# A strided write moves from ScalarE's side of a buffer to VectorE's: key squares and key sum in a quaternion memory kernel

## The chip, the cores and the metric

The kernel runs on one core of a Trainium2 chip. The metric is the device time of one launch, in microseconds. Three runs of the kernel before gave 640.27 us (median; 639.76 to 642.27).

## The reference

Two batches of 4096 tokens with 256 channels pass through three blocks, each adding to the residual: half a feed-forward block, a memory block, and half a feed-forward block again. Of the memory block, cut to what matters here:

```python
keys = (x @ Wk.T + bk).reshape(B, L, 64, 4)              # 64 quaternions of 4 components
knorm = jnp.linalg.norm(keys, axis=-1, keepdims=True)    # root of the sum of the 4 squares
keys = keys / jnp.maximum(knorm, 1e-12)
values = (x @ Wv.T + bv).reshape(B, L, 64, 4)
memory = jnp.cumsum(quat_mul(values, keys), axis=1)      # prefix sum over the tokens
retrieved = quat_mul(memory, quat_conj(keys)).reshape(B, L, D)
retrieved = retrieved / jnp.sqrt(positions)
normed = (retrieved - mean) / jnp.sqrt(var + 1e-5) * ln_g + ln_b   # over the 256 channels
return x + (normed @ Wo.T + bo)
```

## The kernel before

The residual stays in the on-chip memory `res` for the whole run. A feed-forward stage over blocks of 512 tokens comes first, then the memory stage, then a second feed-forward stage. The change is in the memory stage.

The memory stage works in **steps** of 256 tokens (two tiles of 128 tokens, `i` = 0 and 1), alternating between the batches `b` = 0 and 1. Step s = 2j + b; there are 32 of them, s = 0 to 31. `rounds` writes the first four and the last four out and runs the 24 between, s = 4 to 27, in a hardware loop of two steps an iteration. Weights are laid out by component on the host, so the 256 channels of a key stand as four runs of 64: all first components, then all second ones, and so on.

Each engine runs its own list of instructions in order, with semaphores between them. The lists are written out by hand in `body` of each engine; nothing reorders them. In one step, with the line of each:

- TensorE makes the keys and values (L1369) of the step after, the prefix sums of this step (L1398, L1405), and transposes and the output product of the step before (L1414, L1425).
- ScalarE, in `body` under `mem`: copies the key bias (L919), the transposed input (L908), `normedT` (L954) and the value bias (L924), adds the normalized input (L900), squares the keys (`key_square`, L930, `ksq`), takes the layer norm's standard deviation (`std`, L882, `n_std`), takes the norm of the keys (`key_norm`, L937 and L940), and normalizes (L891, L947).
- VectorE, in `body` under `mem`: unit keys (`key_unit`, L616, `khat`), products of tile 0 (`bind`, L622, written to `xn`), retrieval products of tile 0 (`retrieve`, L622, written to `gating_buffers`), statistics of the step before (`ln_stats`, L582), `bind` of tile 1, `own_stats` (L595, L596: a wait for its own statistics, carried by a write of one column that nobody reads), `ln_moments` (L587, two aggregations into `n_mv`), `key_sum` (L603, `ksum`), `store_x` (L659), `ln_inverse` (L592, `n_rstd`), `retrieve` of tile 1, `key_inverse` (L609, `kinv`).
- GpSimd adds the products up, twelve additions a step (L267 to L294).

`ksq` is laid out with the four components of a quaternion beside each other. ScalarE reads the keys component by component and so writes every fourth word of `ksq`, 16 bytes apart; `key_sum` reads it straight through, four words to a sum.

The links that matter: `key_sum` waits for `ksq_done` from ScalarE; `std` on ScalarE waits for `mv_done` from `ln_moments`; `ln_inverse` on VectorE waits for `std_done`, and `retrieve` of tile 1 stands behind it. ScalarE runs `key_square`, `std`, `key_norm` in that order. Steps 1 and 2 have no `store_x`.

Of the kernel before, what the change touches and what calls it, by code (L numbers as in the profile page):

```python
# [21 lines left out]
ALU = mybir.AluOpType  # L22
ACT = mybir.ActivationFunctionType

P = 128
# [5 lines left out]
def need(engine, semaphore, count):  # L31

    if isinstance(count, int) and count <= 0:
        return
    engine.wait_ge(semaphore, count)
# [34 lines left out]
def at(j, b, d):  # L70

    return j + (b + d) // 2, (b + d) % 2


def macaron(nc, x, w_kv, w_o, w_r, w_k, w_v, columns, out):
# [3 lines left out]
    Q = D // 4  # L79
# [8 lines left out]
    with ExitStack() as ctx:  # L88
        def sb(name, shape, dt=F32):
            return ctx.enter_context(nc.sbuf_tensor(name, shape, dt))  # L90

        def sem(name):
            return ctx.enter_context(nc.semaphore(name))
# [70 lines left out]
        n_rstd = sb("n_rstd", [P, 2, 2])  # L164
        m_xn = sb("m_xn", [P, 2, D])
        m_xnT = sb("m_xnT", [P, FC, 2 * P])
        ksq = sb("ksq", [P, 2, Q, 4])
        ksum = sb("ksum", [P, 2, Q])
        above = sb("above", [P, 2, Q])
        knorm = sb("knorm", [P, 2, Q])  # L170
# [21 lines left out]
        keys = bank[0][:, 1, :].rearrange("p (t n) -> p t n", t=2)  # L192
# [45 lines left out]
        m = {n: sem(f"m_{n}") for n in MEM_SEMS}  # L238
# [110 lines left out]
        def _(dve):  # L349
# [208 lines left out]
            def mem():  # L558

                def x_variance(n, first, end):  # L560
                    dve.wait_ge(m["x_moments_done"], 2 * (end // CT))
                    nc.vector.tensor_scalar(x_var[:, :, first:end], x_moments[:, :, first:end, 1], LN_EPS, None,
                                            ALU.add).then_inc(m["x_var_done"], 1)

                def x_scales(n, first, end):
                    if n == 0:
                        dve.wait_ge(m["x_power_done"], 1)
                    else:
                        dve.wait_ge(m["x_std_done"], n)
                        nc.vector.reciprocal(x_rstd[:, :, first:end], x_std[:, :, first:end]).then_inc(m["x_rstd_done"], 1)  # L570
                        dve.wait_ge(m["x_rstd_done"], n)
                    nc.vector.tensor_scalar(x_gain[:, :, first:end], x_rstd[:, :, first:end], 1.0, None, ALU.add)
                    nc.vector.scalar_tensor_tensor(x_shift[:, :, first:end], x_moments[:, :, first:end, 0], -1.0,
                                                   x_rstd[:, :, first:end], ALU.mult, ALU.mult).then_inc(m["x_scales_done"], 1)


                def ln_stats(j, b):
                    s = 2 * j + b
                    need(dve, m["normed_done"], s - 1)
                    for i in range(2):  # L580
                        dve.wait_ge(ret_done[i], s + 1)
                        nc.vector.bn_stats(n_st[:, b, i, :], ret[:, b, i, :]).then_inc(m["st_done"], 1)  # L582

                def ln_moments(j, b):
                    s = 2 * j + b
                    for i in range(2):
                        last = nc.vector.bn_aggr(n_mv[:, b, i, :], n_st[:, b, i, :])  # L587
                    last.then_inc(m["mv_done"], 1)

                def ln_inverse(j, b):  # L590
                    dve.wait_ge(m["std_done"], 2 * j + b + 1)
                    nc.vector.reciprocal(n_rstd[:, b, :], n_std[:, b, :]).then_inc(m["rstd_done"], 1)  # L592

                def own_stats(j, b):
                    dve.wait_ge(m["st_done"], 2 * (2 * j + b) + 2)  # L595
                    nc.vector.memset(spare[:, :], 0.0)  # L596

                def key_sum(j, b):

                    s = 2 * j + b  # L600
                    dve.wait_ge(m["ksq_done"], s + 1)
                    need(dve, m["above_done"], s)
                    nc.vector.tensor_reduce(ksum[:, :, :], ksq[:, :, :, :], mybir.AxisListType.X, ALU.add).then_inc(m["ksum_done"], 1)  # L603

                def key_inverse(j, b):
                    s = 2 * j + b
# [13 lines left out]
                def all_products(dst, b, i, of, done):  # L620

                    nc.vector.tensor_tensor(  # L622
                        dst[:, i, :, :].rearrange("p (a b) n -> p a b n", a=4),
                        of.rearrange("p (a n) -> p a n", n=Q).unsqueeze(2).to_broadcast([P, 4, 4, Q]),
                        khat[:, b, i, :].rearrange("p (b n) -> p b n", n=Q).unsqueeze(1).to_broadcast([P, 4, 4, Q]),
                        ALU.mult).then_inc(done, 1)

                def bind(j, b, i):
                    s = 2 * j + b
                    dve.wait_ge(m["khat_done"], s + 1)  # L630
                    dve.wait_ge(m["V_done"], s + 1)
                    need(dve, bound_done[i], s)
                    all_products(bprod, b, i, values[b][:, i, :], bprod_done[i])

                def retrieve(j, b, i):
                    s = 2 * j + b
                    need(dve, ret_done[i], s)
                    dve.wait_ge(upto_done[i], s + 1)
                    all_products(rprod, b, i, memory[b], rprod_done[i])

                def first_inverse():
                    key_sum(0, 0)
                    key_inverse(0, 0)
# [10 lines left out]
                def store_x(j, b):  # L654
                    s = 2 * j + b
                    dve.wait_ge(m["O_done"], s + 1)
                    dve.wait_ge(m["res_done"], s + 1)
                    t = tiles(b * NT + j * 2, 2)
                    nc.vector.tensor_tensor(t, o_bank, t, ALU.add).then_inc(m["x_done"], 1)  # L659

                def body(j, has, next_stats, next_scales, next_difference):
                    for b in range(2):
                        behind = has(b, -1)
                        if not has(b, 1):

                            retrieve(j, b, 0)
                            store_x(*at(j, b, -3))
                            next_stats(1)
                            retrieve(j, b, 1)
                            ln_stats(*at(j, b, -1))  # L670
                            own_stats(*at(j, b, -1))
                            ln_moments(*at(j, b, -1))
                            store_x(*at(j, b, -2))
                            ln_inverse(*at(j, b, -1))
                            next_difference()
                            continue
                        last_but_one = has(b, 1) and not has(b, 2)
                        if has(b, -1) and not has(b, -2):
                            x_variance(2, NT - CT, NT)
                        if has(b, -2) and not has(b, -3):  # L680
                            x_scales(2, NT - CT, NT)
                        if has(b, 1):
                            key_unit(*at(j, b, 1))
                            bind(*at(j, b, 1), 0)
                        retrieve(j, b, 0)
                        if last_but_one:
                            next_scales(0)
                        if behind:
                            ln_stats(*at(j, b, -1))
                        if has(b, 1):  # L690
                            bind(*at(j, b, 1), 1)
                        if behind:
                            own_stats(*at(j, b, -1))
                            ln_moments(*at(j, b, -1))
                        if has(b, 3) and not has(b, 4):
                            next_stats(0)
                        if has(b, 2):
                            key_sum(j + 1, b)
                        if has(b, -3):
                            store_x(*at(j, b, -3))  # L700
                        if behind:
                            ln_inverse(*at(j, b, -1))
                        retrieve(j, b, 1)
                        if has(b, 2):
                            key_inverse(j + 1, b)
# [58 lines left out]
        def _(act):  # L764
# [109 lines left out]
            def mem():  # L874
# [51 lines left out]
                def key_square(j, b):  # L926
                    s = 2 * j + b
                    act.wait_ge(m["K_done"], s + 1)
                    need(act, m["ksum_done"], s)
                    nc.scalar.activation(ksq[:, :, :, :].rearrange("p t n c -> p t c n"), keys.rearrange("p t (c n) -> p t c n", n=Q),  # L930
                                         ACT.Square).then_inc(m["ksq_done"], 1)

                def key_norm(j, b):
# [633 lines left out]
```

## Time and profile before

| | value |
|---|---|
| Median of three runs | 640.27 us |
| Profiled execution: its own time | 642.52 us |
| Profiled execution: span | 640.8 us |
| Mean granted TensorE clock, share of full speed | 0.991 |
| TensorE busy, share of span | 612.2 us, 96% |
| VectorE busy | 561.6 us, 88% |
| GpSimd busy | 530.6 us, 83% |
| ScalarE busy | 467.8 us, 73% |

The shares are means over three different stages; a stage has to be read by itself. The memory stage lies between about 180 and 470 us of the span, its hardware loop between about 232 and 432 us. Records overlap a little: an instruction's record may start some 0.07 us before the one ahead of it ends, so what an instruction costs its engine is the distance between two starts, not its duration. The span is counted inside the device time, which is 1.7 us longer.

### The profile page before, as it was taken

The numbers are of one execution on the slowest core, as the hardware profiler recorded it, in microseconds if no ns is written. First come the engines' busy times: TensorE is split into PE (matmuls) and PEld (weight loads), VectorE is DVE, ScalarE is ACT, GpSimd is POOL, SyncE is SP. The second block draws the span as 40 slices with busy tenths as digits, with TensorE's granted clock in tenths as the row PEclk, the third lists the DMA queues.
The fourth block names the chain that finished last, engine by engine and source line by source line (L and its number), as shares of the span: only waits on it lengthen the run. The fifth ranks groups of instructions, "written<-read, shape, count | busy, mean of one in ns | idle before, by whom it ended". The sixth has DMA issues, their size and how long they took to land.

```text
span 640.8 us, 12174 instructions
## 1 busy us (share of the span) xinstructions
PE 612.2 (96%) x3294; PEld 517.5 (81%) x3295; DVE 561.6 (88%) x1170; ACT 467.8 (73%) x858; POOL 530.6 (83%) x616
## 2 busy tenths in 40 slices
PE   6899999999997899999999999998899999999997
PEld 4688989989875777877877778777678898898996
DVE  6699999998868999999999999999988788787773
ACT  5576777767656888888888888887476767777662
POOL 1589888887846999999999999998937988889863
PEclk8999999999998999999999999999899999999999
DMA  7840000000000000000000000000000111110221
GB/s 233 256 136 2 0 0 0 0 0 1 1 1 1 0 3 0 0 0 0 0 0 0 0 0 0 0 0 1 1 1 33 35 65 49 50 65 33 66 66 65
DMA packets 19273, 18.65 MB, mean 29 GB/s; under 512 B 1329, under 2 KB 19249, under 8 KB 19249
## 3 DMA queue, kind: packets, MB, share of 16 engines
q1 hardware_dynamic: 19248, 18.36, 8.8%
q8 instruction: 11, 0.18, 0.1%
q14 instruction: 14, 0.11, 0.1%
HBM read 9.97 MB, written 8.39 MB: 29 GB/s over the span
## 4 chain that ended last, share of the span: by engine, by line
PE 49%; POOL 25%; issue 18%; DVE 2%; ACT 2%; DMA 1%; POOLq 1%; SPq 0%; ACTq 0%; DVEq 0%
PE bank L1251 24%; PE bank L1292 17%; POOL rhalf L287 7%; POOL ret L294 6%; POOL kact L276 5%; POOL bhalf L269 4%; PE bank L1265 4%; PE bank L1425 1%; POOL bhalf L267 1%; PE bank L1311 1%; DMA wo<-w_o 1%; POOL rhalf L285 1%; ACT xn L794 1%; PE bank L1242 1%; POOL xr_lo L1108 1%
## 5 line engine op out<-in xcount | busy, mean ns | idle before, releaser
L1292 PE MATMUL bank<-wffn,kact 128*128 128x256 f32 x512 | 117.4, 382 | 4.8 <-DVE kact L425 2.8
L1369 PE MATMUL bank<-wkv,m_xnT 128*128 128x256 f32 x480 | 117.9, 389 | 2.1 <-ACT m_xnT L908 2.1
L301 POOL TENSOR_TENSOR xk_lo<-xk,xk_hi 128x1024 fp32r<-128x1024 f32 x30 | 71.1, 2370 | 47.7 <-ACT xk_hi L810 47.6
L1369 PEld LDWEIGHTS bank<-wkv,m_xnT 128*128 128x128 f32 x480 | 89.9, 192 | 24.3 <-ACT m_xnT L908 8.5
L1292 PEld LDWEIGHTS bank<-wffn,kact 128*128 128x128 f32 x512 | 94.8, 190 | 18.1 <-DVE kact L425 3.2
L1115 POOL TENSOR_TENSOR res<-res,gating_buffers 128x1024 f32 (+1 forms) x31 | 74.6, 2408 | 12.9 <-DVE gating_buffers L432 12.5
L622 DVE TENSOR_TENSOR xn<-bank,khat 128x1024 f32<-128x1024 f32 x64 | 77.7, 1216 | 2.2
L622 DVE TENSOR_TENSOR gating_buffers<-bank,khat 128x1024 f32<-128x1024 f32 x64 | 77.5, 1210 | 0.3 <-POOL ret L294 0.3
L1108 POOL TENSOR_TENSOR xr_lo<-xr,xr_hi 128x1024 fp32r<-128x1024 f32 x30 | 71.1, 2369 | 1.5
L1425 PE MATMUL bank<-wo_centred,normedT 128*128 128x256 f32 x256 | 67.7, 394 | 4.1 <-DVE res L659 2.1
L794 ACT ACTIVATE xn<-res,shift,rstd 128x256 f32 (+1 forms) x124 | 64.4, 594 | 4.6 <-POOL shift L1103 3.6
L1251 PE MATMUL bank<-wffn_hi,xr_hi 128*128 128x256 f32 x240 | 67.4, 281 | 0.0
L1251 PE MATMUL bank<-wffn_hi,xr_lo 128*128 128x256 f32 x240 | 67.4, 281 | 0.0
L1251 PE MATMUL bank<-wffn_lo,xr_hi 128*128 128x256 f32 x240 | 67.3, 280 | 0.0
L1425 PEld LDWEIGHTS bank<-wo_centred,normedT 128*128 128x128 f32 x256 | 44.6, 194 | 22.3 <-issue 14.0
L816 ACT CAST xr_hi<-xr 128x1024 fp32r<-128x1024 f32 x30 | 31.4, 1046 | 38.4 <-DVE xr L417 38.4
L267 POOL TENSOR_TENSOR bhalf<-xn 128x256 f32<-128x256 f32 x64 | 46.8, 731 | 11.2 <-DVE xn L622 11.1
L432 DVE TENSOR_TENSOR gating_buffers<-bank,gating_buffers 128x1024 f32<-128x1024 f32 x31 | 37.7, 1217 | 20.8 <-ACT gating_buffers L833 15.2
L407 DVE TENSOR_TENSOR diff<-bank,xnT 128x1024 f32<-128x1024 f32 x32 | 39.1, 1222 | 15.6 <-ACT xnT L785 15.4
L1251 PE MATMUL bank<-xk_hi,wffn_hi 128*128 128x512 f32 x120 | 50.1, 418 | 0.0
L285 POOL TENSOR_TENSOR rhalf<-gating_buffers 128x256 f32<-128x256 f32 x64 | 47.0, 734 | 2.2 <-DVE gating_buffers L622 2.1
L276 POOL TENSOR_TENSOR kact<-bhalf 128x256 f32<-128x256 f32 x64 | 47.5, 743 | 0.2
(140 smaller groups left out, 1602.0 us busy)
## 6 DMA issues: line engine op xcount, KB each, us to landing
res<-x SPq DMA_DIRECT2D x15, 512.0 KB, 4.2
out<-res SPq DMA_DIRECT2D x15, 512.0 KB, 2.9
res<-x SPq DMA_DIRECT2D x2, 256.0 KB, 2.9
out<-res SPq DMA_DIRECT2D x2, 256.0 KB, 2.1
wffn<-w_k SPq DMA_DIRECT2D x1, 256.0 KB, 5.3
wffn<-w_r SPq DMA_DIRECT2D x1, 256.0 KB, 6.0
wo<-w_o SPq DMA_DIRECT2D x1, 256.0 KB, 6.3
wffn<-w_v SPq DMA_DIRECT2D x1, 256.0 KB, 6.6
```

The lines of the kernel that those rows point to most:

```text
L267: engine.tensor_tensor(quarters(bhalf[:, i, 0, :]), picked(p, BIND_PLUS), picked(p, BIND_MINUS), ALU.subtract)
L276: engine.tensor_tensor(bound[:, b, i, :], bhalf[:, i, 0, :], bhalf[:, i, 1, :], ALU.add).then_inc(bound_done[i], 1)
L285: engine.tensor_tensor(quarters(rhalf[:, i, 0, :]), picked(p, RET_PLUS), picked(p, RET_MINUS), ALU.subtract)
L301: ops.tensor_tensor(xk_lo[:, :, :], xk[:, :, :], xk_hi[:, :, :].bitcast(F32), ALU.subtract).then_inc(e["xklo_done"], 1)
L622: nc.vector.tensor_tensor(dst[:, i, :, :].rearrange("p (a b) n -> p a b n", a=4), of.rearrange("p (a n) -> p a n", n=Q).unsqueeze(2).to_br ...
L794: last = nc.scalar.activation(xn[:, b, i, :], t[:, i, :], ACT.Identity, bias=shift[:, b, i:i + 1], scale=rstd[:, b, i:i + 1])
L1108: nc.gpsimd.tensor_tensor(xr_lo[:, :, :], xr[:, :, :], xr_hi[:, :, :].bitcast(F32), ALU.subtract).then_inc(e["xrlo_done"], 1)
L1115: nc.gpsimd.tensor_tensor(t, t, gated, ALU.add).then_inc(e["res_done"], 1)
L1251: last = nc.tensor.matmul(out_ap, w(f), v(f), start=k == 0, stop=k == n - 1)
L1292: last = nc.tensor.matmul(dst[:, i, :], x[:, f, i * P:(i + 1) * P], wffn[:, w, f, :], start=f == 0, stop=f == FC - 1)
L1369: last = nc.tensor.matmul(dst[:, i, :], m_xnT[:, f, i * P:(i + 1) * P], wkv[:, f, col:col + D], start=False, stop=f == FC - 1, skip_group_ ...
L1425: nc.tensor.matmul(o_bank[:, i, :], normedT[:, f, i * P:(i + 1) * P], wo_centred[:, f, :], start=f == 0, stop=False)
```

## The change

Three things change. `ksq` is laid out component by component: ScalarE now writes four runs of 64 words, and VectorE's reduction reads the four terms of a sum 64 words (256 bytes) apart. In the steps that have a `key_sum` (s = 0 to 29), VectorE runs it ahead of the two aggregations instead of behind them, and the wait for its own statistics stands in front of the sum. In these steps the write of one column (`own_stats`) is gone; steps 30 and 31 keep it.

```diff
--- before.py
+++ after.py
@@ -164,7 +164,7 @@
         n_rstd = sb("n_rstd", [P, 2, 2])
         m_xn = sb("m_xn", [P, 2, D])
         m_xnT = sb("m_xnT", [P, FC, 2 * P])
-        ksq = sb("ksq", [P, 2, Q, 4])
+        ksq = sb("ksq", [P, 2, 4, Q])
         ksum = sb("ksum", [P, 2, Q])
         above = sb("above", [P, 2, Q])
         knorm = sb("knorm", [P, 2, Q])
@@ -600,7 +600,7 @@
                     s = 2 * j + b
                     dve.wait_ge(m["ksq_done"], s + 1)
                     need(dve, m["above_done"], s)
-                    nc.vector.tensor_reduce(ksum[:, :, :], ksq[:, :, :, :], mybir.AxisListType.X, ALU.add).then_inc(m["ksum_done"], 1)
+                    nc.vector.tensor_reduce(ksum[:, :, :], ksq[:, :, :, :].rearrange("p t c n -> p t n c"), mybir.AxisListType.X, ALU.add).then_inc(m["ksum_done"], 1)
 
                 def key_inverse(j, b):
                     s = 2 * j + b
@@ -689,13 +689,17 @@
                             ln_stats(*at(j, b, -1))
                         if has(b, 1):
                             bind(*at(j, b, 1), 1)
+                        if has(b, 2):
+
+                            if behind:
+                                dve.wait_ge(m["st_done"], 2 * (2 * j + b - 1) + 2)
+                            key_sum(j + 1, b)
+                        elif behind:
+                            own_stats(*at(j, b, -1))
                         if behind:
-                            own_stats(*at(j, b, -1))
                             ln_moments(*at(j, b, -1))
                         if has(b, 3) and not has(b, 4):
                             next_stats(0)
-                        if has(b, 2):
-                            key_sum(j + 1, b)
                         if has(b, -3):
                             store_x(*at(j, b, -3))
                         if behind:
@@ -927,7 +931,7 @@
                     s = 2 * j + b
                     act.wait_ge(m["K_done"], s + 1)
                     need(act, m["ksum_done"], s)
-                    nc.scalar.activation(ksq[:, :, :, :].rearrange("p t n c -> p t c n"), keys.rearrange("p t (c n) -> p t c n", n=Q),
+                    nc.scalar.activation(ksq[:, :, :, :], keys.rearrange("p t (c n) -> p t c n", n=Q),
                                          ACT.Square).then_inc(m["ksq_done"], 1)
 
                 def key_norm(j, b):
```

On VectorE, from `bind` of tile 1 to `key_inverse` in the first step of the hardware loop, before (`xn` is what `bind` writes, `gating_buffers` what `retrieve` writes; ISA rows work out semaphore targets and addresses):

```order
L622 TENSOR_TENSOR xn<-bank,khat 128x1024 [waits m_bound1_done,m_V_done,m_khat_done]
L595 ISA
L596 MEMSET spare 128x1 [waits m_st_done]
L587 BN_AGGR n_mv<-n_st 128x2 x2
L601 ISA
L603 TENSOR_REDUCE ksum<-ksq 128x128 [waits m_above_done,m_ksq_done]
L656 ISA
L659 ISA [waits m_res_done,m_O_done]
L659 TENSOR_TENSOR res<-bank,res 128x512
L592 RECIPROCAL n_rstd<-n_std 128x2 [waits m_std_done]
```

And the same place now:

```order
L622 TENSOR_TENSOR xn<-bank,khat 128x1024 [waits m_bound1_done,m_V_done,m_khat_done]
L695 ISA
L601 ISA [waits m_st_done]
L603 TENSOR_REDUCE ksum<-ksq 128x128 [waits m_above_done,m_ksq_done]
L587 BN_AGGR n_mv<-n_st 128x2 x2
L656 ISA
L659 ISA [waits m_res_done,m_O_done]
L659 TENSOR_TENSOR res<-bank,res 128x512
L592 RECIPROCAL n_rstd<-n_std 128x2 [waits m_std_done]
```

The reduction has moved up past the two aggregations and directly behind the products, the column write has gone, and its wait (`m_st_done`) stands at an ISA row ahead of the reduction. Behind the aggregations only `store_x` (L659) is now left ahead of the reciprocal that waits for `m_std_done`. In the changed kernel lines behind the edit have numbers larger by 4.

## Rows read from the trace of the kernel before

**Rows 1.** Hardware loop: stretch, length, busy PE, PEld, DVE, ACT, POOL; clock, DMA share, GB/s.

```profile
232.00:432.00 200.00, 198.64 (x983) 159.78 (x982) 194.84 (x332) 170.66 (x353) 194.80 (x282) 1.00 0.00 0
```

**Rows 2.** Timeline of VectorE, one step: start us, duration us, instruction.

```profile
310.64 0.18 DVE L587 BATCH_NORM_AGGREGATE n_mv<-n_st 128x2 f32<-128x6 f32 x1
310.66 0.06 DVE L596 MEMSET spare<- 128x1 f32 x1
310.74 0.15 DVE L587 BATCH_NORM_AGGREGATE n_mv<-n_st 128x2 f32<-128x6 f32 x1
310.80 0.65 DVE L603 TENSOR_REDUCE ksum<-ksq 128x128 f32<-128x512 f32 x1
311.37 0.68 DVE L659 TENSOR_TENSOR res<-bank,res 128x512 f32 x1
311.97 0.15 DVE L592 RECIPROCAL n_rstd<-n_std 128x2 f32<-128x2 f32 x1
312.04 1.20 DVE L622 TENSOR_TENSOR gating_buffers<-bank,khat 128x1024 f32<-128x1024 f32 x1
313.16 0.94 DVE L609 RECIPROCAL kinv<-knorm 128x128 f32<-128x128 f32 x1
314.14 0.69 DVE L616 TENSOR_TENSOR khat<-bank,kinv 128x512 f32<-128x512 f32 x1
314.95 1.23 DVE L622 TENSOR_TENSOR xn<-bank,khat 128x1024 f32<-128x1024 f32 x1
316.09 1.22 DVE L622 TENSOR_TENSOR gating_buffers<-bank,khat 128x1024 f32<-128x1024 f32 x1
317.22 0.91 DVE L582 BATCH_NORM_STATS2 n_st<-ret 128x6 f32<-128x256 f32 x2
318.05 1.21 DVE L622 TENSOR_TENSOR xn<-bank,khat 128x1024 f32<-128x1024 f32 x1
319.18 0.18 DVE L587 BATCH_NORM_AGGREGATE n_mv<-n_st 128x2 f32<-128x6 f32 x1
```

**Rows 3.** Waits, 240 to 420 us: total us, times, longest us.

```profile
ACT bank L919 <- DVE khat L616: 16.8, 21, 0.8
...
POOL bhalf L267 <- DVE xn L622: 5.0, 22, 0.2
...
PEld bank L1369 <- ACT m_xnT L908: 3.9, 10, 0.4
```

**Rows 4.** Timeline of ScalarE in the same step; idle time before it in brackets.

```profile
309.60 1.13 ACT L930 ACTIVATE ksq<-bank 128x512 f32<-128x512 f32 x1
311.02 0.48 ACT L882 ACTIVATE n_std<-n_mv,eps_pos 128x1 f32<-128x1 f32 x2 [0.28 <-DVE n_mv L587]
311.49 0.40 ACT L937 ACTIVATE above<-ksum,minus_least 128x128 f32<-128x128 f32 x1
...
314.86 0.59 ACT L919 COPY bank<-kv_bias 128x512 f32<-128x512 f32 x1 [0.76 <-DVE khat L616]
```

**Rows 5.** Timeline of VectorE in step 1, which stores no block.

```profile
208.04 0.18 DVE L587 BATCH_NORM_AGGREGATE n_mv<-n_st 128x2 f32<-128x6 f32 x1
...
208.84 0.17 DVE L592 RECIPROCAL n_rstd<-n_std 128x2 f32<-128x2 f32 x1
```

**Rows 6.** ScalarE by line, whole run: busy us, mean ns of one; idle before.

```profile
L930 ACT ACTIVATE ksq<-bank 128x512 f32<-128x512 f32 x32 | 36.2, 1131 | 7.5 <-PE bank L1369 4.8 <-PE bank L1379 1.3
...
L785 ACT COPY xnT<-bank 128x1024 f32<-128x1024 f32 x32 | 32.5, 1016 | 1.7 <-PE bank L1275 0.5 <-PE bank L1265 0.3
...
L908 ACT COPY m_xnT<-bank 128x512 f32<-128x512 f32 x32 | 18.5, 580 | 1.4 <-PE bank L1362 1.4
```

**Rows 7.** VectorE by line, whole run.

```profile
L622 DVE TENSOR_TENSOR gating_buffers<-bank,khat 128x1024 f32<-128x1024 f32 x64 | 77.5, 1210 | 0.3 <-POOL ret L294 0.3
...
L603 DVE TENSOR_REDUCE ksum<-ksq 128x128 f32<-128x512 f32 x32 | 21.0, 656 | 5.6 <-ACT ksq L930 5.6
```

**Rows 8.** Waits of VectorE, whole run: total us, times, longest us.

```profile
DVE ksum L603 <- ACT ksq L930: 5.6, 2, 3.2
```

## Prediction

> **What bounds the kernel now.** I read the split by stretches first, since the change touches only the memory stage. In the 200 us of its hardware loop four engines look full [rows 1]: TensorE 198.64 us, GpSimd 194.80, VectorE 194.84; ScalarE, with 170.66, is the only one with room. Busy shares don't tell which of them paces, so next come the waits. Over 21 steps GpSimd waits for VectorE's products 22 times, 5.0 us in all, 0.23 us a step; ScalarE waits for the unit keys 21 times, 16.8 us, 0.8 us a step; TensorE's weight loads wait for ScalarE's copy, 3.9 us in all [rows 3]. No wait of VectorE is long enough to be listed. The timeline confirms it: from 310.64 to 319.18 VectorE starts one instruction after another, each at most 0.13 us after the end of the one ahead and most of them a little before it [rows 2]. So a step is 8.54 us long because VectorE's list is that long, and the loop has 24 steps. What lengthens VectorE's list by d costs 24 d there; what shortens ScalarE's buys nothing while it still waits 0.8 us a step. GpSimd follows closely: if VectorE were quicker, at most 0.23 us a step could be had before GpSimd paces.
>
> **The squares on ScalarE.** Writing every fourth word, the square of 128x512 takes 1131 ns; a copy of the same size out of PSUM that writes straight takes 580 ns [rows 6]. The new write is straight, so I expect about 590 ns, 0.55 us less on each of 32. In the loop this buys nothing: ScalarE's next instruction, the standard deviation, waits for VectorE's aggregations anyway (idle 0.28 us even now, [rows 4]). Where VectorE waits for the squares it is a gain: that happens twice, outside the loop [rows 8], so -1.1 us.
>
> **The sum on VectorE.** It now reads words 256 bytes apart. No row shows VectorE doing that, so its cost is bounded. Lower end: nothing, 656 ns as now [rows 7], if VectorE is held only by its count of elements; a gain is excluded, since count, output and engine are the same. Upper end: all that the same 512 elements cost ScalarE extra when they were 16 bytes apart, 1131 - 580 = 0.55 us [rows 6]. Between them stands a limit per access: ScalarE's straight word costs (1016 - 580) / 512 = 0.85 ns, its spaced word 0.85 + 551 / 512 = 1.93 ns [rows 6]. VectorE's straight word costs (1210 - 690) / 512 = 1.02 ns [rows 2, 7]. Were each spaced word to cost 1.93 ns here too, the sum would grow by 512 x 0.91 ns = 0.47 us. The nearest row is the spaced write, the only spaced access in the trace; I take 0.40 us, a little under, since VectorE reads four words for each that it writes while ScalarE wrote every one. Times 32 sums: +12.8 us. VectorE paces the 24 steps of the loop; in the eight sums outside it the sum stands on the path too, ahead of the key norm at the start and in a full list of VectorE elsewhere.
>
> The Trainium skill (Vector Engine (DVE) Microarchitecture Reference, Measured stream behaviour on trn2) speaks against this edit: a port streams at full rate only in runs of two adjacent words, and one source that hops at every element took 1.73 ns a column where contiguous ones took 1.054. An estimate by that is 512 x 0.68 ns = 0.35 us a sum, and the whole would come to 654.4 us instead of my 656. The same section has a one-source operation that alternates between two regions and still reads at full rate; by that one the sum would cost nothing. Neither was measured on a reduction, and no row here decides between them.
>
> **The order on VectorE, and the new wait.** Let R be the start of the sum. It takes the place of the first aggregation, 1.13 us behind the start of the second product (318.05 to 319.18, [rows 2]). It holds VectorE 0.57 us (310.80 to 311.37), each aggregation about 0.08, so `store_x` starts at R + 0.73 and the reciprocal `n_rstd` could start 0.60 later, at R + 1.33. That is what the list gives now as well: first aggregation to reciprocal 311.97 - 310.64 = 1.33. But the reciprocal waits for ScalarE's standard deviation, which waits for the second aggregation. Now the sum lies beside that round trip and hides it: from first aggregation to the end of the deviations 311.50 - 310.64 = 0.86 us [rows 2, 4]. After the change the first aggregation starts at R + 0.57; with 0.02 less for the column write and 0.04 for the release (314.10 to 314.14, `kinv` to `khat`) the reciprocal can't start before R + 0.57 + 0.86 - 0.02 + 0.04 = R + 1.45. So VectorE has a new wait of 0.12 us a step, and behind it stands `retrieve` of tile 1, then the reciprocal of the norms, `khat` and all of the next step: 24 x 0.12 = +2.9 us. A slower sum doesn't change this term, since it moves both sides.
>
> Steps 1 and 2 have no `store_x`. There first aggregation to reciprocal is 208.84 - 208.04 = 0.80 us [rows 5], already the round trip; with the sum ahead it becomes 0.57 + 0.80, so +0.57 us each, +1.1 us. In step 28 the statistics of the next stage stand between, and nothing is added. Steps 3 and 29 I put at nothing.
>
> **The column write.** Its record is 0.06 us, but the aggregations around it start at 310.64 and 310.74 [rows 2], so it holds VectorE 0.02 at most. In the loop that is already in the chain above, whose end decides. I cost it at nothing otherwise. Its wait for the statistics costs nothing either: these end before the second product starts, 1.13 us earlier.
>
> **What moves on the other engines.** The key norm gets its sum 0.16 us earlier but stands behind the deviations on ScalarE, which end later: 0.56 us later against the start of the product in the free case, and 0.96 with the slower sum, while `khat` itself moves by 0.12 or 0.52. ScalarE's 0.76 us of idle time ahead of the bias copy [rows 4] falls to about 0.3 in either case, so nothing behind it is late. The edit of the order pays back nothing there.
>
> **The sum.** 12.8 + 2.9 + 1.1 - 1.1 = +15.7 us. The profiled execution took 642.52 us itself (span 640.8 and 1.7 around it), so its like would take 658.2. It lies 2.25 us above the median of the three runs, 640.27; taken off, the forecast is 656.0 us, 2.5% slower.
>
> **The rivals.**
> 1. The spaced read is free. For it: an engine that takes one word a cycle may fetch far enough ahead; the spaced access that was slow was a write. Against it: the write was slowed to about twice. Left are 2.9 + 1.1 - 1.1 = +2.9 us, 643.2 us, +0.45%. That is so near the 0.5% (3.2 us) a measurement of this kernel can tell from no change that I split it two to one between same and slower.
> 2. The loop is paced by a ring and not by VectorE's list: unit keys, bias copy, transposed copy, key product, squares, key sum. For it: the squares end at 310.73, only 0.07 us ahead of the sum at 310.80 [rows 2, 4]. If that edge is the true limit, 0.55 us off the squares frees the step until GpSimd paces, which has 0.23 us to give [rows 3]: 24 x 0.23 = 5.5 us, and 634.8 us. It decides wherever VectorE idles ahead of the sum and the read is free. Against it: VectorE doesn't idle there, the aggregation ahead runs right up to the sum.
> 3. The spaced read costs far more than the spaced write did, 0.8 us a sum: 32 x 0.8 + 2.9 = +28.5, 668.8 us. Against it: no row has a word of 2.6 ns.
> 4. The order does not matter because ScalarE answers faster (its two deviations start at once): rival 1 or the forecast less 2.9 us, within their ranges.
>
> **Chances and range.** Forecast 0.57, rival 1 0.31, rival 2 0.05, rival 3 0.07. The likeliest case alone, with 0.25 to 0.55 us a sum, spans 8.0 to 17.6 us and the 2.9: 651 to 661 us. The range has to take in the free read and the upper bound: 641 to 662. From the cases: faster by over 0.5% 0.06, within 0.5% 0.22, slower 0.72.
>
> **What would show it.** In the changed profile: the squares at about 590 ns; the mean of the key sum, 656 ns if rival 1 holds, 1.0 to 1.1 us if I am right; idle time of VectorE ahead of `n_rstd` put down to ScalarE's deviations, about 0.1 us in each of 24 steps; step length 8.54 + 0.12 + 0.40 = 9.06 us in the loop (8.66 with a free read). GpSimd's wait for products should grow by the same amount a step. I am wrong if the key sum keeps its time, if no wait appears ahead of `n_rstd`, or if the step gets shorter than 8.54 us.

## The result, and the profile after

The changed kernel took 658.78 us (median of six; 656.92 to 661.98) against 640.43 us for six runs of the kernel before. The medians are 18.4 us apart, where 15.7 had been forecast. The ratio of the runs is 1.027, 95% interval 1.025 to 1.029, which is 17.2 us (15.8 to 18.6); 18.4 lies inside, and a remainder of a microsecond or two is not resolved by it. The profiled execution took 661.98 us itself, span 660.3, and is the slowest of the six; its mean granted clock was 0.982 where the other five had 0.988 or 0.989. That matters below.

The memory stage holds nearly all of it. From the start of the first `khat` to the start of the last it took 452.34 - 185.38 = 266.96 us before, and 470.54 - 184.53 = 286.01 us now. The hardware loop's 24 steps grew from 8.54 to 9.08 us each.

The loop's stretch in the changed profile, columns as in [rows 1]; it is now 219 us long:

```profile
232.00:451.00 219.00, 206.60 (x1019) 164.62 (x1018) 211.90 (x314) 160.31 (x362) 200.98 (x290) 1.00 0.00 0
```

ScalarE is down to 160.31 us in a longer stretch, GpSimd has 200.98 of 219; VectorE, with 211.90, is the fullest. One step of VectorE, which answers to [rows 2]:

```profile
318.67 1.04 DVE L603 TENSOR_REDUCE ksum<-ksq 128x128 f32<-128x512 f32 x1
319.64 0.23 DVE L587 BATCH_NORM_AGGREGATE n_mv<-n_st 128x2 f32<-128x6 f32 x2
319.80 0.65 DVE L659 TENSOR_TENSOR res<-bank,res 128x512 f32 x1
320.51 0.17 DVE L592 RECIPROCAL n_rstd<-n_std 128x2 f32<-128x2 f32 x1
320.60 1.22 DVE L622 TENSOR_TENSOR gating_buffers<-bank,khat 128x1024 f32<-128x1024 f32 x1
321.73 0.94 DVE L609 RECIPROCAL kinv<-knorm 128x128 f32<-128x128 f32 x1
322.71 0.69 DVE L616 TENSOR_TENSOR khat<-bank,kinv 128x512 f32<-128x512 f32 x1
323.52 1.23 DVE L622 TENSOR_TENSOR xn<-bank,khat 128x1024 f32<-128x1024 f32 x1
324.67 1.22 DVE L622 TENSOR_TENSOR gating_buffers<-bank,khat 128x1024 f32<-128x1024 f32 x1
325.80 0.91 DVE L582 BATCH_NORM_STATS2 n_st<-ret 128x6 f32<-128x256 f32 x2
326.62 1.21 DVE L622 TENSOR_TENSOR xn<-bank,khat 128x1024 f32<-128x1024 f32 x1
327.75 1.04 DVE L603 TENSOR_REDUCE ksum<-ksq 128x128 f32<-128x512 f32 x1
```

From sum to sum it is 327.75 - 318.67 = 9.08 us. The sum holds VectorE 0.97 us (318.67 to 319.64) instead of 0.57, and `store_x` to `n_rstd` is 0.71 us (319.80 to 320.51) instead of 0.60: the reciprocal waits. ScalarE in the same step, which answers to [rows 4]:

```profile
317.63 0.60 ACT L934 ACTIVATE ksq<-bank 128x512 f32<-128x512 f32 x1
320.00 0.48 ACT L886 ACTIVATE n_std<-n_mv,eps_pos 128x1 f32<-128x1 f32 x2 [1.76 <-DVE n_mv L587]
320.39 0.39 ACT L941 ACTIVATE above<-ksum,minus_least 128x128 f32<-128x128 f32 x1
...
323.44 0.59 ACT L923 COPY bank<-kv_bias 128x512 f32<-128x512 f32 x1 [0.44 <-DVE khat L616]
```

The squares are quick and buy nothing: they are followed by 1.76 us of waiting for the aggregations. The deviations end at 320.48, and `n_rstd` starts 0.03 us later. The idle time ahead of the bias copy fell from 0.76 us to 0.44, where the prediction had about 0.3. By line, the two operations whose access was exchanged, squares first ([rows 6, 7] before):

```profile
L934 ACT ACTIVATE ksq<-bank 128x512 f32<-128x512 f32 x32 | 19.2, 599 | 9.6 <-PE bank L1373 7.1 <-PE bank L1383 1.3
```

```profile
L603 DVE TENSOR_REDUCE ksum<-ksq 128x128 f32<-128x512 f32 x32 | 33.4, 1044 | 5.9 <-ACT ksq L934 4.6 <-issue 1.4
```

ScalarE gave back 1131 - 599 = 532 ns a step, VectorE's record grew by 1044 - 656 = 388 ns. Not all of the 388 is the read: the experiments show that some 20 ns come with the sum's new place. The waits, 240 to 430 us, against [rows 3]:

```profile
ACT n_std L886 <- DVE n_mv L587: 37.3, 21, 1.8
...
POOL bhalf L267 <- DVE xn L622: 15.8, 21, 0.8
...
PE bank L1429 <- DVE res L659: 8.7, 21, 0.4
```

GpSimd's wait for VectorE's products is up from 0.23 to 0.75 us a step, the 0.5 us by which the list of VectorE grew. TensorE now waits for `store_x` (L1429, 0.4 us a step), which it did not before; it costs nothing by itself, as the experiments leave no third term in the loop. VectorE's new wait ahead of `n_rstd` is too short for this view: outside steps 1 and 2 it shows only in the distances between starts, 0.71 against 0.60 us.

### The profile page after: what moved, and what is told of

It reads as the page before. It is cut to its first block, busy times and chain, and to the rows that moved or that the text cites. A ratio compares the mean times of both kernels' runs of the same rounds, so it can differ in the third digit from the quotient of the medians.

```text
span 660.3 us, 12145 instructions
## 1 busy us (share of the span) xinstructions
PE 620.1 (94%) x3294; PEld 521.2 (79%) x3295; DVE 576.6 (87%) x1141; ACT 447.7 (68%) x858; POOL 530.9 (80%) x616
## 4 chain that ended last, share of the span: by engine, by line
PE 47%; POOL 26%; issue 18%; DVE 4%; ACT 2%; DMA 1%; POOLq 1%; SPq 0%; DVEq 0%; ACTq 0%
PE bank L1255 23%; PE bank L1296 16%; POOL rhalf L287 6%; POOL bhalf L269 6%; POOL ret L294 6%; POOL kact L276 5%; PE bank L1269 4%; PE bank L1429 1%; POOL bhalf L267 1%; PE bank L1315 1%; POOL rhalf L285 1%; DMA wo<-w_o 1%; PE bank L1246 1%; DVE diff L407 1%; ACT xn L798 0%
## 5 line engine op out<-in xcount | busy, mean ns | idle before, releaser
L1373 PE MATMUL bank<-wkv,m_xnT 128*128 128x256 f32 x480 | 119.5, 393 | 4.6 <-ACT m_xnT L912 2.1
L1296 PE MATMUL bank<-wffn,kact 128*128 128x256 f32 x512 | 119.2, 387 | 4.8 <-DVE kact L425 2.8
L1429 PE MATMUL bank<-wo_centred,normedT 128*128 128x256 f32 x256 | 69.7, 403 | 13.2 <-DVE res L659 12.6
L1429 PEld LDWEIGHTS bank<-wo_centred,normedT 128*128 128x128 f32 x256 | 45.8, 199 | 31.7 <-issue 23.2
L407 DVE TENSOR_TENSOR diff<-bank,xnT 128x1024 f32<-128x1024 f32 x32 | 39.1, 1222 | 16.0 <-ACT xnT L789 15.8
L886 ACT ACTIVATE n_std<-n_mv,eps_pos 128x1 f32<-128x1 f32 x64 | 15.4, 287 | 55.4 <-DVE n_mv L587 55.3
```

The source lines that it names most:

```text
L407: nc.vector.tensor_tensor(diff[:, :, :], xT_ps, xnT[:, b, :, 0:CW], ALU.subtract).then_inc(e["diff_done"], 1)
L1296: last = nc.tensor.matmul(dst[:, i, :], x[:, f, i * P:(i + 1) * P], wffn[:, w, f, :], start=f == 0, stop=f == FC - 1)
L1373: last = nc.tensor.matmul(dst[:, i, :], m_xnT[:, f, i * P:(i + 1) * P], wkv[:, f, col:col + D], start=False, stop=f == FC - 1, skip_group_ ...
L1429: nc.tensor.matmul(o_bank[:, i, :], normedT[:, f, i * P:(i + 1) * P], wo_centred[:, f, :], start=f == 0, stop=False)
```

## Experiments

The theory after the result: the spaced read costs 0.39 us a sum and the new wait some 0.12 us a step, and the two add up. The rivals: the read alone does it; the order does most of it; an engine behind them paces. Loop steps below are the mean distance of the starts of `khat` over the 24 steps. Edits are shown shortened. The kernel before was run again beside each group of experiments: its median was 642.05 us (17 runs) beside the first four (layout, order, late reciprocal, pairs) and 641.00 us (23 runs) beside the others, against the 640.4 that the first expectations start from. The ratios are to these runs.

**The layout alone.**

```diff
-        ksq = sb("ksq", [P, 2, Q, 4])
+        ksq = sb("ksq", [P, 2, 4, Q])
-  tensor_reduce(ksum[:, :, :], ksq[:, :, :, :], X, ADD)
+  tensor_reduce(ksum[:, :, :], ksq[:, :, :, :].rearrange("p t c n -> p t n c"), X, ADD)
-  activation(ksq[:, :, :, :].rearrange("p t n c -> p t c n"), keys..., Square)
+  activation(ksq[:, :, :, :], keys..., Square)
```

> Only the layout of ksq is changed; order and column write as before. Theory (the spaced read costs 0.39 us a sum, the order a further 0.12 us a step): 640.4 + 32 x 0.39 - 1.1 for the faster squares = 651.8 us, key sum 1.04 us, no idle time ahead of n_rstd, loop step 8.54 + 0.39 = 8.93 us. Rival A (the spaced read alone makes all of the loss): 658.8 us. Rival B (the order makes most of it): under 648 us.

Measured: 652.77 us, ratio 1.015 (1.012 to 1.019); step 8.91 us, 0.37 above the kernel before. VectorE's timeline:

```profile
315.77 1.02 DVE L603 TENSOR_REDUCE ksum<-ksq 128x128 f32<-128x512 f32 x1
316.70 0.68 DVE L659 TENSOR_TENSOR res<-bank,res 128x512 f32 x1
317.30 0.16 DVE L592 RECIPROCAL n_rstd<-n_std 128x2 f32<-128x2 f32 x1
```

The sum is slow, and the reciprocal follows `store_x` after 0.60 us as before: no wait. The sum holds VectorE 0.93 us (315.77 to 316.70) in the place where it held it 0.57. Both rivals fall: the step carries 0.37 of the 0.54 us, neither all nor the smaller part, and 652.8 is neither 658.8 nor under 648.

**The order alone.**

```diff
-  own_stats; ln_moments; key_sum
+  wait st_done; key_sum; ln_moments          # in steps 0 to 29; layout of ksq as before
```

> Only the order on VectorE is changed and the column write left out; ksq laid out as before, squares 1.13 us, key sum 0.66 us. Theory: n_rstd waits for ScalarE's deviations, and the sum, now earlier, waits a little for the slow squares as well (they end 0.07 us ahead of its old place): loop step about 8.70 us, 24 x 0.16 + 1.1 for steps 1 and 2 = +5, 645.4 us. Rival A (the spaced read is all of the loss): 640.4 us or a little under, from the write that is gone.

Measured: 651.94 us, ratio 1.015 (1.012 to 1.019). The expectation was 6.5 us too low, 1.6 of which is the kernel before, which took 642.05 in this round and not 640.4. The step is 8.84 us, 0.30 more than before, and the place where it comes from is in VectorE's timeline:

```profile
322.73 1.21 DVE L622 TENSOR_TENSOR xn<-bank,khat 128x1024 f32<-128x1024 f32 x1
323.96 0.69 DVE L603 TENSOR_REDUCE ksum<-ksq 128x128 f32<-128x512 f32 x1
324.56 0.24 DVE L587 BATCH_NORM_AGGREGATE n_mv<-n_st 128x2 f32<-128x6 f32 x2
324.72 0.66 DVE L659 TENSOR_TENSOR res<-bank,res 128x512 f32 x1
325.45 0.17 DVE L592 RECIPROCAL n_rstd<-n_std 128x2 f32<-128x2 f32 x1
325.53 1.22 DVE L622 TENSOR_TENSOR gating_buffers<-bank,khat 128x1024 f32<-128x1024 f32 x1
```

Product to sum is 1.23 us (1.13 before): the sum waits for the slow squares. Sum to reciprocal is 1.49 us, 0.16 above the 1.33 of before. So the order costs more with the old layout than with the new, and the two costs do not simply add: 0.37 and 0.30 alone make 0.54 together, because the layout takes the wait for the squares away. The estimate of 0.16 a step was to hold both waits, which measure 0.10 and 0.16; the last 0.04 lie in the rest of the list.

**The reciprocal moved out of the way.**

```diff
   store_x
-  ln_inverse
   retrieve(j, b, 1)
+  ln_inverse
   key_inverse                                # the rest as in the changed kernel
```

> The changed kernel with the reciprocal n_rstd moved behind the retrieval of tile 1, so that it no longer stands where ScalarE's answer is late. Theory: the new wait of 0.11 us in 24 steps and 0.55 us in steps 1 and 2 goes, -3.7 us: 655.1 us, loop step 8.97 us. Rival C (the wait hides a slower engine behind it, TensorE's new wait for store_x or GpSimd): no change, 658.8 us.

Measured: 651.84 us, ratio 1.015 (1.012 to 1.019), 1.1% under the changed kernel by the two ratios, give or take 0.4%. The step is 8.90 us, 0.19 less than in the changed kernel and 0.02 less than with the layout alone. In the timeline `retrieve` now follows `store_x` after 0.57 us:

```profile
318.17 0.66 DVE L659 TENSOR_TENSOR res<-bank,res 128x512 f32 x1
318.74 1.22 DVE L622 TENSOR_TENSOR gating_buffers<-bank,khat 128x1024 f32<-128x1024 f32 x1
319.88 0.16 DVE L592 RECIPROCAL n_rstd<-n_std 128x2 f32<-128x2 f32 x1
```

So the order costs nothing in the loop once its one wait is gone; rival C falls. The traces account for 24 x 0.19 = 4.6 us in the loop and 1.1 in steps 1 and 2, 5.7 where 3.7 had been expected. The 7 us or so between the times of the two kernels, which were not run side by side, have an uncertainty of nearly 3 us, so they show no further gain.

**Pairs.** Nothing said yet why the read is slow. Here the old order is kept and `ksq` holds pairs of neighbouring words.

```diff
-        ksq = sb("ksq", [P, 2, Q, 4])
+        ksq = sb("ksq", [P, 2, 2, Q, 2])
-  tensor_reduce(ksum[:, :, :], ksq[:, :, :, :], X, ADD)
+  tensor_reduce(ksum[:, :, :], ksq[...].rearrange("p t h n c -> p t n h c"), XY, ADD)
-  activation(ksq[:, :, :, :].rearrange("p t n c -> p t c n"), keys..., Square)
+  activation(ksq[...].rearrange("p t h n c -> p (t h) c n"), keys..., Square)
```

> Order and column write as before; ksq laid out in pairs, components 0 and 1 of each key side by side, then 2 and 3: ScalarE writes every second word, VectorE reads runs of two words, 128 words apart. Theory (VectorE pays for reading single words that stand apart): key sum back at 0.66 us, squares between 0.6 and 1.1 us; the loop gains nothing from ScalarE, so 639.3 to 640.4 us. Rival D (any step in the reduction's operand costs, also between pairs): key sum 0.8 us or more, 645 us or more.

Measured: 640.20 us (12 runs), ratio 0.997 (0.995 to 1.000). By line:

```profile
L603 DVE TENSOR_REDUCE ksum<-ksq 128x128 f32<-128x512 f32 x32 | 21.0, 655 | 4.8 <-ACT ksq L930 4.8
L930 ACT ACTIVATE ksq<-bank 128x512 f32<-128x512 f32 x32 | 20.9, 652 | 7.7 <-PE bank L1369 5.0 <-PE bank L1379 1.3
```

Reading pairs 128 words apart costs VectorE nothing (655 ns); writing every second word costs ScalarE 652 ns, not 1131. The sum is now taken over two axes (XY) where it was over one (X), and is as quick, so that costs nothing either. And the step stays at 8.54 us although the squares lost 0.48 us: this time of ScalarE's is worth nothing in the loop, and the ring through the squares (rival 2 of the prediction) doesn't pace it.

**Pairs with the new order**, so that both accesses are quick and the wait is left alone. The edit is the changed kernel's order with the layout above.

> The new order without the column write, with ksq in pairs: both the read of the sum and the squares should be quick, so that the new wait for ScalarE's deviations is left alone. Theory (the wait is 0.12 us a step, and what follows a waiting instruction starts some 0.03 us later): loop step 8.54 + 0.15 = 8.69 us, 3.6 us in the loop and 1.1 in steps 1 and 2, less 1.1 for the squares: +3.6 us against the kernel before, 0.6%. Rival E (the order costs 10 us whatever the layout, as it did with the slow squares): +9 us or more, step 8.84 us.

Measured: 646.95 us (12 runs), ratio 1.008 (1.005 to 1.010), step 8.71 us, 0.17 above before. VectorE's timeline:

```profile
314.20 0.68 DVE L603 TENSOR_REDUCE ksum<-ksq 128x128 f32<-128x512 f32 x1
314.80 0.24 DVE L587 BATCH_NORM_AGGREGATE n_mv<-n_st 128x2 f32<-128x6 f32 x2
314.95 0.66 DVE L659 TENSOR_TENSOR res<-bank,res 128x512 f32 x1
315.68 0.17 DVE L592 RECIPROCAL n_rstd<-n_std 128x2 f32<-128x2 f32 x1
315.76 1.22 DVE L622 TENSOR_TENSOR gating_buffers<-bank,khat 128x1024 f32<-128x1024 f32 x1
```

`store_x` to reciprocal is 0.73 us, sum to reciprocal 1.48. This is the order's own price in the loop. The rival of 9 us falls. The medians lie 6 us apart; the ratio makes it 4.8 us (3.1 to 6.5), which has the 3.6 expected inside it. Set beside runs of like granted clock, the difference is 3.8 and 3.9 us, near the 3.6: seven runs have mean clocks of 0.985 to 0.989 and take 648.2 us in the mean (five such runs of the kernel before: 644.5), and five have 0.993 to 0.997 and take 644.4 (twelve of the kernel before: 640.5). The low clock is commoner here, seven of twelve runs against five of 23; that the order is its cause is not shown.

This run also gives the price of the read alone. Its sum stands where that of the changed kernel stands and takes 676 ns a record (at 655 in the old place, with the same layout). So like for like the single words cost 1044 - 676 = 368 ns in the new place and, from the layout alone, whose sum takes 1022 ns, 1022 - 656 = 366 ns in the old one: 0.37 us and not 0.39. The two rows, pairs with the new order and the layout alone:

```profile
L603 DVE TENSOR_REDUCE ksum<-ksq 128x128 f32<-128x512 f32 x32 | 21.6, 676 | 4.5 <-ACT ksq L934 3.1 <-issue 1.4
```

```profile
L603 DVE TENSOR_REDUCE ksum<-ksq 128x128 f32<-128x512 f32 x32 | 32.7, 1022 | 4.8 <-ACT ksq L930 4.7
```

**Pairs, the new order, and the late reciprocal.**

> As the run with pairs and the new order, with the reciprocal n_rstd behind the retrieval of tile 1. Theory: no cost is left and the column write is saved, step 8.52 us, 1 to 2 us under the kernel before. Rival (the key sum ahead of the aggregations costs by more than this wait): 2 us or more above it.

Measured: 641.61 us (12 runs), ratio 1.000 (0.997 to 1.002). The step is 8.53 us. No cost is left, and the 1 to 2 us hoped for don't show in the time either. Of the versions only the pairs in the old order lie below the kernel before, by 0.3% (interval 0.0 to 0.5%), at the edge of what can be told.

**Distance of the terms.** The changed kernel with the four runs 256 words apart:

```diff
-        ksq = sb("ksq", [P, 2, 4, Q])
+        ksq = sb("ksq", [P, 2, 4, 256])            # words 0 to 63 of each are used
```

> The changed kernel with the four runs of ksq 256 words apart instead of 64, so that the sum's four terms stand 1 KiB apart. Theory (each single word that isn't next to the one before costs the same extra, however far): key sum 1.04 us. Rival F (the extra depends on the distance): below 0.9 or above 1.2 us.

```profile
L603 DVE TENSOR_REDUCE ksum<-ksq 128x128 f32<-128x512 f32 x32 | 33.4, 1043 | 4.4 <-ACT ksq L934 4.4
```

And with the terms 4 words apart, in blocks of 4 keys:

```diff
-        ksq = sb("ksq", [P, 2, 4, Q])
+        ksq = sb("ksq", [P, 2, Q // 4, 4, 4])
+  tensor_reduce(ksum "p t (a e) -> p (t a) e", ksq "p t a c e -> p (t a) e c", X, ADD)
+  for t in range(2): activation(ksq[:, t] "p a c e -> p c a e", keys[:, t] "p (c a e) -> p c a e", Square)
```

> The changed kernel with ksq in blocks of 4 keys: the sum reads its four terms 4 words (16 bytes) apart, the distance at which ScalarE's write took 0.55 us more; ScalarE writes runs of 4 words, now as two instructions of 256 elements. Theory (what counts is that the word stands alone): key sum 1.04 us; squares 0.5 us each, that is unslowed. Rival G (a read within a few neighbouring lines is cheap): key sum near 0.66 us. Rival H (close spacing is the costly one, as ScalarE's 1.08 ns a word was): 1.2 us.

```profile
L603 DVE TENSOR_REDUCE ksum<-ksq 128x128 f32<-128x512 f32 x32 | 33.9, 1058 | 6.1 <-ACT ksq L935 4.7 <-issue 1.4
...
L935 ACT ACTIVATE ksq<-bank 128x256 f32<-128x256 f32 x64 | 21.1, 381 | 9.1 <-PE bank L1375 6.5 <-PE bank L1385 1.3
```

One run of each was made, 661.23 and 662.31 us; their traces are what counts here. The sum takes 1043 ns at 1 KiB and 1058 ns at 16 bytes, against 1044 at 256 bytes: rivals F, G and H fall. ScalarE's squares were expected at 0.5 us each and took 381 ns. That is what a straight write would take: an estimate from 598 ns for 512 elements and the 0.85 ns an element of [rows 6] is 380. So runs of four words cost ScalarE nothing visible.

## Why the prediction was right, step by step

**VectorE paces the loop: right.** But for the wait ahead of `n_rstd` its list is gapless in the changed kernel as well, a shorter square leaves the step at 8.54 us (pairs), and each of its own costs appears in the step in full.

**The spaced read: right in kind and nearly in size.** 0.40 us a sum was taken; 0.37 were measured, in either place of the sum and in the step with the layout alone. The limit per access that was worked out from ScalarE's write gave 0.47 and was too high: VectorE pays 368 / 512 = 0.72 ns a word, ScalarE paid 532 / 512 = 1.04. That the value chosen came closer than the derivation was a choice and not knowledge, and part of it is luck: 0.03 too much for the read and 0.05 too little for the wait below leave 0.52 us a step against 0.54 measured. The upper end, 0.55, would have been a poor forecast. Of the two rules quoted from the Trainium skill (Vector Engine (DVE) Microarchitecture Reference, Measured stream behaviour on trn2), the one of single words that hop (0.35 us a sum) came within 0.02 us, nearer than the 0.40 taken, and its condition, that pairs of adjacent words are free, is what the pairs showed; the full rate of the one-source operation doesn't hold for this reduction.

**The new wait: right in place, a little low in size.** 0.12 us a step was predicted. The reciprocal was predicted at R + 1.45 with a quick sum; it comes at R + 1.48 in the pairs with the new order, and in the changed kernel at 320.51 - 318.67 = 1.84, which less the 0.37 of the read is 1.47. What was missed is small change: a sum directly behind the product holds VectorE 0.60 us where it held it 0.57 behind the aggregations, and what follows the reciprocal adds some 0.02. In all 0.17 us a step (pairs with the new order), 4.1 us instead of 2.9. That the wait is for ScalarE's answer is shown by the late reciprocal, which takes it away and gives the time back. One reading beside it was off and without effect: the statistics end at 318.13 (317.22 + 0.91), just behind the start of the second product at 318.05 and not before it, still a microsecond ahead of the sum.

**Steps 1 and 2: right, and TensorE's clock was left out.** VectorE's idle time ahead of `n_rstd` there is 0.55 us each, as worked out. Not foreseen was a fall of TensorE's granted clock in the steps behind them. Three stretches of the changed profile, columns as in [rows 1]:

```profile
208.00:212.00 4.00, 1.80 (x11) 1.11 (x10) 3.42 (x9) 3.05 (x9) 4.00 (x6) 1.00 0.00 0
212.00:216.00 4.00, 3.25 (x12) 2.15 (x11) 3.96 (x6) 2.62 (x6) 2.04 (x4) 0.57 0.00 0
216.00:220.00 4.00, 4.00 (x12) 3.23 (x11) 2.58 (x4) 1.07 (x2) 4.00 (x7) 0.57 0.00 0
```

and two of the same stretches before:

```profile
208.00:212.00 4.00, 2.55 (x15) 1.78 (x14) 3.97 (x12) 3.29 (x10) 4.00 (x7) 1.00 0.00 0
212.00:216.00 4.00, 3.33 (x17) 2.64 (x16) 3.91 (x7) 3.21 (x7) 3.41 (x6) 1.00 0.00 0
```

Between 208 and 212 us TensorE is busy 1.80 us of 4 (2.55 before); then its granted clock is 0.57 of full speed, so most of the stretch is at the lower level of 1.2 GHz, where before all of it was at 2.4. Its products come late and the squares wait for them on ScalarE (1.88 us), then VectorE for the squares, 1.36 us that the view puts down to issue:

```profile
218.36 0.60 ACT L934 ACTIVATE ksq<-bank 128x512 f32<-128x512 f32 x1 [1.88 <-PE bank L1373]
```

```profile
216.48 1.21 DVE L622 TENSOR_TENSOR xn<-bank,khat 128x1024 f32<-128x1024 f32 x1
219.04 1.06 DVE L603 TENSOR_REDUCE ksum<-ksq 128x128 f32<-128x512 f32 x1 [1.36 <-issue]
```

Near 460 us VectorE waits another 1.36 us, for TensorE; the granted clock is 0.79 and 0.78 from 456 to 464 us. It is as low in the kernel before there (0.78 and 0.80), but by then that kernel is past its last `khat`, at 452.34. After step 2 the fall is also in the profile of the pairs with the new order (0.50, in steps of 10.40 and 9.99 us), but not in the one with the terms 1 KiB apart (1.00 from 212 to 220 us), which has the same waits.

It is tempting to blame VectorE's waits in steps 1 and 2 for it, and the traces don't bear that out. The layout alone (first line) and the late reciprocal (0.58) have no wait ahead of `n_rstd` and have the fall; the order alone (second line) has both waits of 0.55 us and hasn't:

```profile
212.00:216.00 4.00, 3.58 (x13) 2.33 (x12) 3.96 (x6) 2.58 (x6) 2.72 (x5) 0.62 0.00 0
```

```profile
212.00:216.00 4.00, 3.08 (x18) 2.27 (x17) 3.93 (x8) 2.81 (x7) 2.73 (x5) 1.00 0.00 0
```

Nor does TensorE's work in the stretch ahead sort them: it was busy 2.33 us of 4 in the first and 2.11 in the second. What decides it is open. It is not there in every launch of kernels with the same waits, and so may be part of the spread between launches.

**Where the time comes from.** The loop: 24 x 0.54 = 13.0. The eight other sums, if each counts in full: 8 x 0.37 = 3.0. Steps 1 and 2: 1.1. The squares where VectorE waits for them: -1.1, twice 0.5. That makes 16.0; the forecast had 15.7 by 12.8 + 2.9 + 1.1 - 1.1. A kept trace checks this sum. The profile with the terms 1 KiB apart has the same sums and waits, and no fall of the clock between about 202 us and its last `khat`. From first `khat` to last it takes 469.98 - 186.89 = 283.09 us, 16.1 more than the kernel before; this stretch leaves out the first sum and the first squares, which nearly cancel. The changed kernel's own profile has 286.01, and 2.75 of the 2.9 us on top are in two steps, those of the clock's fall: 10.32 and 10.19 us, where the other has 8.87 and 8.89. So in that launch, the slowest of the six, the slower TensorE cost about 2.8 us in the memory stage. The launches that make the median were not traced, so what is left of 17.2 or 18.4 us above the 16.0 is not assigned to anything by a measurement.

**The rivals.** 1 (free read) fell with the key sum's 1044 ns, 2 (ring) with the pairs, 3 (0.8 us a sum) with the same 1044. Rival 4 supposed that ScalarE would answer faster; first aggregation to the end of the deviations is 320.48 - 319.64 = 0.84 us, as the prediction had it.

## What to carry to other kernels

When a strided access has to be on one side of a buffer, put it on the engine that waits, not on the one whose list is the step, even if it costs more nanoseconds there: ScalarE's 532 ns were free and VectorE's 370 were not. Before choosing a side, look for a layout between the two. With pairs VectorE reads two neighbouring words at a time, which cost it nothing, and ScalarE writes every second word, which cost it 54 ns over a straight write (652 against 598). In this kernel it gained little, 0.3% at the edge of what can be told, because ScalarE's time had been free before. And an instruction moved ahead on a full engine moves back whatever another engine is waiting for: count the round trip behind it, and move the instruction that waits for the answer as well.

## What the runs showed of the hardware

VectorE's reduction over fp32 took 0.72 ns a word more when each word read stood alone, and the distance made next to no difference: directly behind a product, 1058 ns at 16 bytes, 1044 at 256, 1043 at 1 KiB, and 676 for pairs 512 bytes apart. Behind the aggregations it took 1022 ns at 256 bytes, 655 for pairs and 656 read straight, so its place in the list was worth 20 ns a record. ScalarE, writing from PSUM, took 1131 ns for words 16 bytes apart, 652 for words 8 bytes apart and 598 for straight ones. And TensorE's granted clock fell in the same part of the stage in some launches and not in others: 0.57 behind a stretch in which TensorE was busy 1.80 us of 4, 0.62 behind one of 2.33, and 1.00 behind one of 2.11. No run here shows what decides it.
